# Rows to the experts by gathers from a slot table built on TensorE, and the combine by accumulating transfers

## The reference

```python
probs  = softmax(top2(logits))                       # logits = x @ router_w + router_b
pos    = rank of the pick within its expert          # cumsum of one-hot over first, then second picks
einp   = zeros(E, cap, C).at[ei, pos].add(x twice)   # a pick with pos >= cap is left out
h, g   = einp @ w_c_fc + b_c_fc, einp @ w_gate + b_gate
o      = silu(h * g) @ w_c_proj + b_c_proj
ffn    = sum over the two picks of probs * o[ei, pos]  # a pos past the end reads the last row
x = x + 0.5 * ffn(layernorm(x))
x = x + attention(layernorm(x))
x = x + 0.5 * ffn(layernorm(x))
```

## Time and profile before

| | us |
|---|---|
| median of 3 runs | 2362.4 |
| lowest and highest | 2360.11, 2366.91 |
| the profiled execution's own time | 2361.27 |
| its span | 2359.5 |
| its mean granted TensorE clock | 0.947 of full |

### The profile page before, as it was taken

The page is one execution under the profiler, slowest core; times in us unless marked ns, Lnnn a source line. Parts: engine busy times, 40 slices in busy tenths (PEclk is TensorE's granted clock), DMA queues, the critical chain, the costliest instruction groups (busy, mean ns, idle before and its releaser), DMA issues.

```text
span 2359.5 us, 37052 instructions
## 1 busy us (share of the span) xinstructions
PE 2005.5 (85%) x13127; PEld 1706.8 (72%) x13128; DVE 1415.8 (60%) x3224; ACT 1019.3 (43%) x1798; POOL 263.9 (11%) x267
## 2 busy tenths in 40 slices
PE   5159999999995999999999999870799999999860
PEld 5148888888884877877778777770688888888660
DVE  6335665566555758668686695653455555666452
ACT  1045666656463433334333333210555665666420
POOL 1620000000002100101001000027000000000524
PEclk9999999999997999999999999955899999999985
DMA  6242221222122000000000000014222222222204
GB/s 261 89 160 81 98 81 62 72 98 98 41 86 66 19 5 13 18 0 18 9 9 18 0 0 1 1 36 148 86 81 63 80 72 80 88 75 83 81 31 138
DMA packets 95354, 150.12 MB, mean 64 GB/s; under 512 B 9583, under 2 KB 76678, under 8 KB 94068
## 3 DMA queue, kind: packets, MB, share of 16 engines
q1 hardware_dynamic: 83008, 116.46, 14.5%
q0 software_dynamic: 12288, 32.91, 4.4%
...
## 4 chain that ended last, share of the span: by engine, by line
PE 69%; DVE 12%; issue 11%; POOL 3%; ACT 1%; another core or an unknown queue 1%; SPq 1%; DMA 1%; DVEq 0%; POOLq 0%
PE bank L574 32%; PE bank L324 13%; PE bank L326 7%; PE bank L641 5%; PE bank L665 4%; DVE wide L1329 2%; POOL halves L469 2%; PE bank L555 2%; PE bank L710 1%; PE bank L714 1%; DVE wide L1331 1%; DVE wide L1301 1%; DVE halves L1357 1%; DVE wide L1315 1%; PE bank L682 1%
## 5 line engine op out<-in xcount | busy, mean ns | idle before, releaser
L574 PE MATMUL bank<-halves 128*128 128x512 f32 (+2 forms) x3744 | 767.3, 365 | 22.5 <-issue 18.1
L574 PEld LDWEIGHTS bank<-halves 128*128 128x128 f32 x3744 | 645.3, 190 | 130.5 <-issue 27.1
L324 PE MATMUL bank<-halves 128*128 128x512 f32 (+1 forms) x1352 | 480.7, 399 | 15.7 <-DVE halves L1357 11.4
L326 PE MATMUL bank<-halves 128*128 128x256 f32 (+1 forms) x1352 | 379.0, 280 | 0.0
L828 ACT ACTIVATE temp<-bank,bias_now 128x512 f32<-128x512 f32 (+1 forms) x312 | 200.3, 642 | 360.9 <-PE bank L574 345.3
L1164 DVE SCALAR_TENSOR_TENSOR temp<-bank,bias_fc,temp 128x512 f32<-128x512 f32 (+1 forms) x312 | 216.0, 692 | 219.7 <-ACT temp L828 214.9
L324 PEld LDWEIGHTS bank<-halves 128*128 128x128 f32 (+1 forms) x1352 | 252.1, 186 | 81.7 <-DVE halves L1357 13.5
L641 PE MATMUL bank<-halves 128*128 128x512 f32 x1152 | 286.3, 400 | 2.0 <-issue 2.0
L1171 DVE TENSOR_TENSOR halves<-temp,halves 128x512 fp32r<-128x512 f32 (+1 forms) x312 | 198.0, 635 | 126.4 <-ACT halves L781 121.8
L326 PEld LDWEIGHTS bank<-halves 128*128 128x128 f32 (+1 forms) x1352 | 253.5, 188 | 0.4
L641 PEld LDWEIGHTS bank<-halves 128*128 128x128 f32 x1152 | 212.0, 189 | 50.0 <-issue 2.4
...
## 6 DMA issues: line engine op xcount, KB each, us to landing
expert_out<-rows SPq DMA_DIRECT2D x144, 128.0 KB, 1.7
...
wide<-expert_in SPq DMA_DIRECT2D x32, 512.0 KB, 4.8
...
out_x<-x SPq DMA_DIRECT2D x32, 128.0 KB
```

What stands on the lines that cost most here:

```text
L324: nc.tensor.matmul(out_, a[0][:, k, of], v[:, k].rearrange("p a n -> p (a n)"), start=(k == 0), stop=False, skip_group_check=True)
L326: ins = nc.tensor.matmul(out_[:, 0:C], a[1][:, k, of], v[:, k, 0, :], start=False, stop=(k == last), skip_group_check=True)
L574: m = pe.matmul(bank[at + b][:, 0:w], a[:, kc, j * P:(j + 1) * P], v[:, kc, 0:w], start=(i == 0), stop=(i == len(ps) - 1))
```

## The change

**Routing.** The normalised rows xn are stored in order to xn_rows in DRAM by SP, four times 1 MB. Nothing is scattered; expert_in, its clearing and expert_out are gone. A table of 8 x 10 slot tiles by 128 slots is made instead, which says for each slot the token that it holds. A slot number is split into its tile (column) and its place in it (low). match on DVE compares both with all 80 tiles and all 128 places, for 8 picks a partition in each of four chunks and 16 in each of two. ACT multiplies the first comparison by the partition's number, POOL by the pick's number, and 64 matmuls of PE (invert) add up both over all picks. From the sums DVE makes three tables of row numbers: x_index, y_index, weight_index.

**Expert inputs.** POOL gathers each slot tile's rows by x_index from xn_rows (gather_rows), ten indirect DMAs for each expert, and by ten more of 128 single numbers the slots' weights (gather_weights). The groups now run in the order 204, 512, 512 columns; the conditional one is first. The next expert's first two groups are turned between the y tiles of this one.

**Combine.** y_out gets a third operation, which multiplies the tile by its slots' weights into a ring of four tiles. POOL adds the tile to rows of DRAM by an accumulating indirect DMA with y_index (add_rows): in round 0 to sum_rows, a copy of the input made by a DMA from DRAM to DRAM, in round 1 to the output, into which x was stored by supertiles after the attention. Before the attention x is loaded back from sum_rows by eight DMAs, each waited for. Slots without a pick are skipped by their number.

**Dropped picks.** A pick past the capacity gets its expert's last row. Each expert stores that row (store_last); in the last expert 16 small DMAs make a table of them, and 16 jobs of two float32 matmuls (add_dropped) multiply it by a turned matrix of the dropped weights. The jobs' results are copied by ACT and DVE in turn to eight staging tiles, and POOL adds each, 256 KB, to the rows of two tiles.

The diff, cut to its core:

```diff
--- before.py
+++ after.py
-GROUPS = [(s, min(512, CAP - s)) for s in range(0, CAP, 512)]
...
+GROUPS = [(1024, CAP - 1024), (0, 512), (512, 512)]
...
+            def store_xn(r, q):
+                sp.wait_ge(xn_made, r * TILES + (q + 1) * QT)
+                sp.dma_start(xn_rows[q * QT * P:(q + 1) * QT * P, :].rearrange(tok, p=P),
+                             xn[:, q * QT:(q + 1) * QT, :]).then_inc(xn_stored, 16)
...
+            def store_last(r, e):
...
-                n = t // 4 if t < 8 else 2
...
-                sp.dma_start(expert_out[bass.ds(at, m), :], y_sb[0:m, t % 2, :]).then_inc(y_stored[t % 2], 16)
+                sp.wait_ge(y_summed, u * Y_TILES + 2)
+                sp.dma_start(last_rows[bass.ds(e, 1), :], y_sb[CAP - 1 - 1024 - P:CAP - 1024 - P, 1, :]).then_inc(last_stored, 16)
...
+            def load_table(r):
+
+                sp.wait_ge(last_stored, (r + 1) * E * 16)
+                sp.wait_ge(table_cleared, r + 1)
+                for n in range(SUPER):
+                    for m in range(SUPER):
+                        at = 32 * n + E * m
+                        sp.dma_start(last_table[at:at + E, m, :], last_rows[:, :]).then_inc(table_loaded, 16)
...
+                if r == 0:
+                    sp.dma_start(sum_rows[:, :], x_in[0]).then_inc(rows_begun, 16)
+                sp.wait_ge(weights_made, r + 1)
+                sp.dma_start(weight_rows.rearrange("(p j) a -> p (j a)", p=P), weights[:]).then_inc(weights_stored, 16)
...
-            with sp.Fori(0, TILES) as i:
...
-                sp.dma_start(out[0, bass.ds(i * P, P), :], x[:, bass.ds(i, 1), :].rearrange("p a c -> p (a c)")).then_inc(stored, 16)
...
+                if r == 0:
+                    for s in range(NSUP):
+                        i = s * SUPER
+                        sp.dma_start(x[:, i:i + SUPER, :],
+                                     sum_rows[i * P:(i + SUPER) * P, :].rearrange(tok, p=P)).then_inc(x_back, 16)
+                        sp.wait_ge(x_back, (s + 1) * 16)
...
+            def by_pick(r, n):
...
+                pool.wait_ge(matched, r * CHUNKS + n + 1)
+                nc.gpsimd.tensor_tensor(by_column[:, picks, COLS:2 * COLS], matches[n],
+                                        pick_ranks[:, picks].unsqueeze(2).to_broadcast([P, picks.stop - picks.start, COLS]),
+                                        ALU.mult).then_inc(by_pick_made, 1)
...
+            def gather_rows(r, e, n):
...
+                for i in range(len(GROUP_TILES[n])):
+                    col = e * Y_TILES + GROUPS[n][0] // P + i
+                    pool.indirect_dma_start(xg[buf][:, i, :], None, xn_rows,
+                                            bass.IndirectOffsetOnAxis(ap=x_index[:, col:col + 1], axis=0)
+                                            ).then_inc(xg_loaded[buf], 16)
...
+            def gather_weights(r, e):
...
+                for i in range(Y_TILES):
+                    col = e * Y_TILES + i
+                    pool.indirect_dma_start(slot_weight[:, col:col + 1], None, weight_rows,
+                                            bass.IndirectOffsetOnAxis(ap=weight_index[:, col:col + 1], axis=0)
+                                            ).then_inc(weight_got, 16)
...
+            def add_rows(r, e, tiles):
...
+                    pool.wait_ge(y_weighted, u * Y_TILES + t + 1)
+                    pool.indirect_dma_start((sum_rows, out[0])[r],
+                                            bass.IndirectOffsetOnAxis(ap=y_index[0:m, col:col + 1], axis=0),
+                                            weighted[0:m, t % RING, :], None, bounds_check=T - 1, oob_is_err=False,
+                                            compute_op=ALU.add).then_inc(y_added[t % RING], 16)
...
+            def add_jobs(r):
...
+                for n in range(JOBS):
+                    i = JOB_TILES[n]
+                    pool.wait_ge(job_copied[n % 2], r * JOBS // 2 + n // 2 + 1)
+                    pool.dma_start((sum_rows, out[0])[r][i * P:(i + 2) * P, :].rearrange(tok, p=P),
+                                   staged[:, n % 8, :].rearrange("p (a c) -> p a c", c=C),
+                                   accum_op=ALU.add).then_inc(job_added[n % 8], 16)
+                for n in range(8):
+                    pool.wait_ge(job_added[n], (r + 1) * JOBS // 8 * 16)
...
-                for n, (k, first, tiles) in enumerate(BLOCKS):
-                    pool.wait_ge(slots_made, r * len(BLOCKS) + n + 1)
...
-                        pool.indirect_dma_start(expert_in,
-                                                bass.IndirectOffsetOnAxis(ap=write_slot[:, j:j + 1], axis=0),
-                                                xn[:, i, :], None, bounds_check=ROWS - 1,
-                                                oob_is_err=False).then_inc(scattered[i // QT], 16)
...
-                            gather(got4[:, i % SUPER, k, :], k, i, rows_got[i % SUPER])
...
-                    for i in range(TILES):
...
+                for n in range(CHUNKS):
+                    by_pick(r, n)
+                pool.wait_ge(x_index_made, r + 1)
...
+                gather_rows(r, 0, 0)
+                gather_rows(r, 0, 1)
+                pool.wait_ge(index_made, r + 1)
+                pool.wait_ge(weights_stored, (r + 1) * 16)
+                gather_weights(r, 0)
+                for e in range(E):
+                    gather_rows(r, e, 2)
+                    if e == 0:
...
+                    else:
+                        landed(r, e - 1, Y_TILES)
+                    add_rows(r, e, range(2))
+                    if e + 1 < E:
+                        pool.wait_ge(xg_turned, (r * E + e) * NG + 3)
+                        gather_rows(r, e + 1, 0)
+                        gather_rows(r, e + 1, 1)
+                        gather_weights(r, e + 1)
+                    else:
+                        landed(r, e, 2)
+                        add_jobs(r)
+                    add_rows(r, e, range(2, Y_TILES))
...
+                def invert(r):
...
+                    for n in range(CHUNKS):
+                        pe.wait_ge(low_matched, r * CHUNKS + n + 1)
+                        pe.wait_ge(by_partition_made, r * CHUNKS + n + 1)
+                        pe.wait_ge(by_pick_made, r * CHUNKS + n + 1)
+                        for j in range(chunk(n).start, chunk(n).stop):
+                            m = pe.matmul(bank[0][:, 0:2 * COLS], by_low[n][:, j - chunk(n).start, :], by_column[:, j, :],
+                                          start=(j == 0), stop=(j == PICKS - 1))
+                    m.then_inc(inverted, 1)
...
+                    if last and n == 2 and j >= 2:
+                        add_dropped(r, 2 * (j - 2))
+                        add_dropped(r, 2 * (j - 2) + 1)
...
+            def add_dropped(r, n):
...
+                if n < 2:
+                    pe.wait_ge(xt_split, (r * E + E) * NG)
+                else:
+                    pe.wait_ge(job_copied[n % 2], r * JOBS // 2 + n // 2)
+                for k in range(2):
+                    m = pe.matmul(bank[6 + n % 2][:, k * C:(k + 1) * C], dropped_turned[at:at + 32, h, :],
+                                  last_table[at:at + 32, (i + k) % 4, :], start=True, stop=True)
+                m.then_inc(job_done, 1)
...
-                up(r, e, 0, first)
-                turn(r, e, 1)
-                up(r, e, 0, second)
...
-                up1(first)
-                turn(r, e, 2)
-                up1(second)
-                down(r, e, 0)
+                wide2 = fills_group(pe, e)
...
+                if last:
+                    turn_dropped(r)
                 with pe.If(last_group):
-                    up(r, e, 2, range(HJ))
+                    up(r, e, 0, range(HJ))
                 with pe.Else():
-
                     pe.drain().then_inc(up_done, HJ)
-                down(r, e, 1, range(2))
+                up(r, e, 1, first)
+                turn(r, e, 2, last)
+                up(r, e, 1, second)
+                with pe.If(last_group):
+                    down(r, e, 0)
...
+                with pe.If(wide2):
+                    up(r, e, 2, range(HJ), last)
+                with pe.Else():
+                    up(r, e, 2, range(HJ), last, NARROW)
+                down(r, e, 1, range(1))
+                if last:
+                    add_dropped(r, 12)
+                    add_dropped(r, 13)
+                down(r, e, 1, range(1, 2))
+                if last:
+                    add_dropped(r, 14)
+                    add_dropped(r, 15)
+                else:
+                    turn(r, e + 1, 0)
+                down(r, e, 1, range(2, 4))
                 if not last:
...
+                        if last and unit >= 2 * HJ + 2:
+                            copy_job(r, 2 * (unit - 2 * HJ - 2))
...
+            def match(r, n):
...
+                v.tensor_tensor(matches[n], tile_ranks[:].unsqueeze(1).to_broadcast([P, m, COLS]),
```

(14 more changed lines are left out.)

476 lines of the change are left out of this document (275 added, 201 removed).

## The result

The changed kernel takes 2617.84 us (median of 4 runs, 2613.16 to 2624.19) where the kernel before takes 2364.65 us (4 runs) beside it: **1.107 times as long, 95% interval 1.104 to 1.111**, so 253 us slower. Forecast were 2295 us, 66 us faster, with 2375 us as the upper end. The sign was wrong, and the size even more.

The account below looks back on a forecast made before the run. PE was taken to bound the experts, uncovered queues of small POOL transfers the routes and tail. Terms from -69 (tail) to +58 (last experts) summed to -66.5 against 2361.3: 2295 us, range 2250 to 2375.

Parts of the forecast that it names:

- the two routes: Routing stages: matching and gathers replace scatters, -20 in the first with +4 for expert 0's third load, -28 in the second.
- the tail: Behind the last matmul: 76.4 us become 9 us with a little room, -69 (-60 to -71).
- the start of the attention: PE's wait before the attention, now for reloaded x: 17.5 us instead of 24.2, -6.5 (-12 to +5).
- the attention: Attention stage: DVE loses 64 additions of the combine, but PE is the busy engine, -3 (0 to -8).
- the row of 10.40 us: Old tail's first gather, 10.40 us instead of 0.95; if a price after pauses, the new tail would save only 59.
- Expert loops: Both rounds' experts: third DVE operation covered, only new joints cost, +12 for 16 experts (0 to 20).
- own sign of being wrong: Experts: prediction wrong if PE's busy sum differs from 1177 us plus 23 by more than 20.
- The lag: Rival, looped experts: POOL's back-to-back indirect transfers cost PE 6.92 us each, +97, 2392 us in all; chance 0.17.
- it decides: Looped experts: delays from POOL's back-to-back indirect transfers decide the outcome from 5 us in each expert (66.5 / 14).
- Last expert: Each round's last expert: dropped-pick jobs 11.5, copy waits 12.5, table 5; +29 a round (15 to 35), +58 in all.
- the lag that went: Second round's last expert: no burst of 32 gathers any more, so its delay goes, -14 (0 if jobs bring it too).
- The second rival: Jobs' accumulating transfers take 3 us instead of 1.7, last ten y tiles wait, 2340 us; chance 0.10.

Follow-up runs that it names:

- the shorter runs: Changed kernel with the ten weight gathers issued in two pieces of five, so at most 8 indirect POOL DMAs in a row instead of 18: 2473.16 us.
- best: Changed kernel with weight gathers in fives, y tiles later on DVE, no branch wait, earlier job copy, two more joint edits: 2344.9 us, 0.994 times the kernel before.
- the four causes: Long unbroken POOL DMA sequences, y-tile order on DVE, DVE's branch, late even-job copy; changed kernel with all four edited: 2351.08 us.

## Why the prediction was wrong

**Right:** the two routes (-18.4 and -28.1 where -16 and -28 stood), the tail (-64.1 for -69; its own 9 us would have made it -67), the start of the attention (-4.2 for -6.5) and the attention (-2.9 for -3). PE waits for its first rows 28.5 us in four waits now. By term the first route was only right in sum, which was luck: POOL's product of 1280 elements takes 4.3 us and not 1.4, and DVE's comparison beside it 3.6 us instead of 1.5, and yet the gathers start at 106.88, 9 us earlier than worked out. The first rows then come later. The sixth gather's issue ends at 114.8, PE's turn of them is at 120.70 and its first matmul of a unit at 128.78, so 5.9 and 8.1 us pass where 1.8 and 4.1 stood. Two of its sums slip without effect: 129.3 - 4 + 2 is 127.3, and a chunk's two operations come to 2.05 us by its own rows and not 1.9. No transfer on POOL in the new tail waits: nothing of the row of 10.40 us came back. That fits DVE's run of 12.74 us beside it as its price, as the Trainium skill (SBUF — State Buffer, "SBUF: two separate sides") has it. The longest indirect transfer of POOL's is 2.39 us, and two direct ones take 2.44.

**The step that failed is "Expert loops", +12 us (0 to 20).** It measured +301 (from the first expert's start to the last one's: 487.8 to 641.1 us and 514.3 to 662.2). The prediction's own sign of being wrong came true with it: PE's busy sum in the experts is 1329 us, where 1177 + 23 within 20 was asked for. Three things were wrong in the step.

1. *The lag was put down as a rival with a chance of 0.17 and not as part of the forecast*, although showed it in three bursts. The argument against it, that a burst of 16 stood beside DVE's work without it (row of 753.99), was no argument: PE computed nothing at that time, so no matmul's signal could be late. That weight gathers move 512 bytes and not 128 KB spoke for the opposite: small ones cost more. The rival's own price, 6.92 us an expert and 97 in all, was short of the 139 that the shorter runs gave back, since it left out the clock: of the 145 us that the experts then got shorter, 94 are PE's idle time, close to its 97, and 51 PE's busy time. The bound used for "it decides" (5 us an expert) was passed.
2. *The joints were priced by today's waits*, 18.1 us in 11 waits, "two thirds as much again". But the new order has its own waits, which the order of the instructions showed before any run: two y tiles on DVE ahead of the product for which PE's third unit waits, with no y tiles' matmuls to cover them in experts without a last group; and DVE's branch at the start of an expert. Each is mostly 3.0 to 4.1 us, in 16 and in 8 experts; taken away singly they gave 45 and 23 us, in part by the clock, and in part they came back elsewhere.
3. *"DVE is busy 347 of 582 us, so it is covered"* is an average. What counts is what stands between a matmul and the next one that needs its result, there and then.

Even in best, without the four causes, the loops measure +67 (521.2 and 548.1 us) and not +12. Where those come from in detail no run here shows.

**"Last expert", +29 a round (15 to 35), came out at +43.5 in the first** (93.9 to 137.4 us) and +34 in the second (103.0 to 136.7), or +48 if the lag that went (-14) is added. PE's wait for ACT's copy was right (2.5 forecast, 2.53 measured, five times a round), and so was its cause; a job's matmul takes 0.39 us for 0.36. PE waits for the table 2.1 and 1.9 us where 5 stood. What was missed is the clock again and the wait of the third group.

**Direction of the range.** The range's upper end took the lower half of one rival alone. The four causes together are 257 us, none of which was in the forecast but for the 25 of the copies.

The second rival (slow accumulating transfers) was right in kind: they are slower still, 5.5 us to the landing where it supposed 3. Its effect was small: the jobs as a whole, with these transfers, cost 22 us a round in best.
